# One spreading product per unit instead of two: stacking the high and low parts of the combine weights in a two-layer tower kernel

## What is computed

```python
scores = einsum('btd,de->bte', x, router_w)              # 16 experts
probs = softmax(scores)
routing_weights, routing_idx = top_k(probs, 2)
routing_weights = routing_weights / sum(routing_weights)
combine = einsum('btk,btke->bte', routing_weights, one_hot(routing_idx))   # token x 16, two nonzeros
g = einsum('btd,edf->ebtf', x, gate_w)                   # F = 192 hidden columns an expert
u = einsum('btd,edf->ebtf', x, up_w)
h = silu(g) * u
expert_out = einsum('ebtf,efd->ebtd', h, down_w)
out = einsum('ebtd,bte->btd', expert_out, combine)
```

## Time and profile before

| | |
|---|---|
| median of 3 runs | 296.05 us (294.83 to 296.13) |
| profiled execution | 296.34 us, of which the span is 294.5 us |
| PE busy | 273.1 us, 93% of the span, 1813 matmuls |
| DVE busy | 238.0 us, 81% |
| ACT busy | 147.0 us, 50% |
| POOL busy | 10.0 us, 3% |
| mean granted TensorE clock | 0.984 of full |

### The profile page before, as it was taken

One profiled execution on the slowest core, in us unless ns is written; L12 is line 12 of the kernel. 1 busy time (PEld: TensorE's weight loads), 2 busy tenths in 40 slices (PEclk: granted clock), 3 DMA queues, 4 the chain that ended last, 5 costly groups with the idle time before them and its releaser, 6 DMA issues. The chain is left out here.

```text
span 294.5 us, 4710 instructions
## 1 busy us (share of the span) xinstructions
PE 273.1 (93%) x1813; PEld 237.4 (81%) x1816; DVE 238.0 (81%) x441; ACT 147.0 (50%) x238; POOL 10.0 (3%) x30
## 2 busy tenths in 40 slices
PE   8789399979999999999999999977999999999993
PEld 3445265869999999999999989766899989999862
DVE  1969998897996999899898856799668895878683
ACT  2898750106655664555655433322147773673630
POOL 0200000020000000000000005000000000000000
PEclk9999959999999999999999999999999999999998
DMA  6950499916171755546300085094000000000003
GB/s 234 419 213 19 146 364 434 425 76 212 49 277 26 298 164 189 221 146 240 115 0 3 0 323 249 16 378 178 0 2 0 0 3 0 2 1 2 0 0 71
DMA packets 6567, 40.47 MB, mean 137 GB/s; under 512 B 1169, under 2 KB 1425, under 8 KB 5266
## 3 DMA queue, kind: packets, MB, share of 16 engines
q1 hardware_dynamic: 6546, 40.18, 36.4%
HBM read 39.13 MB, written 0.52 MB: 135 GB/s over the span
## 5 line engine op out<-in xcount | busy, mean ns | idle before, releaser
L876 PE MATMUL bank<-s_xt_hi,s_gu_hi 128*128 128x256 f32 x120 | 34.0, 283 | 0.0
L877 PE MATMUL bank<-s_xt_lo,s_gu_hi 128*128 128x256 f32 x120 | 33.9, 283 | 0.0
L878 PE MATMUL bank<-s_xt_hi,s_gu_lo 128*128 128x256 f32 x120 | 33.9, 282 | 0.0
L994 PE MATMUL bank<-s_xf_hi,s_f_lo 128*128 128x256 f32 x128 | 31.1, 281 | 0.0
L994 PE MATMUL bank<-s_xf_hi,s_f_hi 128*128 128x256 f32 x128 | 31.1, 281 | 0.0
L459 ACT CAST s_xt_hi<-bank 128x512 fp32r<-128x512 f32 x10 | 5.9, 587 | 40.6 <-PE bank L668 34.9
L1515 DVE TENSOR_TENSOR s_f_lo<-s_ffn_raw,s_f_hi 128x1024 fp32r<-128x1024 f32 x16 | 19.6, 1225 | 6.1 <-ACT s_f_hi L592 6.1
L994 PEld LDWEIGHTS bank<-s_xf_hi,s_f_hi 128*128 128x128 f32 x128 | 24.1, 188 | 0.4
L994 PEld LDWEIGHTS bank<-s_xf_hi,s_f_lo 128*128 128x128 f32 x128 | 24.1, 188 | 0.3
L877 PEld LDWEIGHTS bank<-s_xt_lo,s_gu_hi 128*128 128x128 f32 x120 | 23.0, 191 | 0.2
L876 PEld LDWEIGHTS bank<-s_xt_hi,s_gu_hi 128*128 128x128 f32 x120 | 23.0, 191 | 0.3
(11 more groups left out here) (253 smaller groups left out, 713.1 us busy)
## 6 DMA issues: line engine op xcount, KB each, us to landing
s_moe_raw<-moe_gu SPq DMA_DIRECT2D x16, 768.0 KB, 5.9
s_ffn_raw<-ffn_w SPq DMA_DIRECT2D x4, 2048.0 KB, 9.8
s_moe_raw<-moe_dn SPq DMA_DIRECT2D x8, 768.0 KB, 4.4
s_big_raw<-att_w SPq DMA_DIRECT2D x4, 1024.0 KB, 8.7
s_big_raw<-down_w SPq DMA_DIRECT2D x1, 4096.0 KB, 25.2
s_l_raw<-l_w SPq DMA_DIRECT2D x1, 2560.0 KB, 15.2
out<-s_h SPq DMA_DIRECT2D x4, 128.0 KB, 2.3
s_tok_w<-tok_w SPq DMA_DIRECT2D x1, 256.0 KB, 2.7
```

What stands on the lines that cost most here:

```text
L876: pe.matmul(dst, w_hi, xt_hi[:, k, :], start=(k == 0), stop=False)
L877: pe.matmul(dst, w_hi, xt_lo[:, k, :], start=False, stop=False)
L878: last = pe.matmul(dst, w_lo, xt_hi[:, k, :], start=False, stop=(k == KC - 1))
L994: pe.matmul(tb(j, n)[:, 0:TOK], M[w][j][:, k, n * P:(n + 1) * P], M["xf_hi"][:, k, :], start=(w == "w_hi" and k == 0), stop=False)
```

## The change

The high and the low part of the combine matrix are put into different rows of one tile `ct`: high in rows 0 to 15, low in rows 32 to 47 (`CT_LOW = 32`). For this the last routing operation writes the combine matrix three times beside each other (`top3`, 48 columns a tile), so that the transpose delivers it in rows 0 to 15, 16 to 31 and 32 to 47. ACT rounds all 48 rows, DVE replaces rows 32 to 47 by the rest. `ident_r` gets a second one in each column, 32 rows lower, and `sel` is copied from it. Rows 16 to 31 meet only zeros. One matmul then sums high and low part.

```diff
+        CT_LOW = 32
...
-                B["top"] = sb("top", [P, 8, TILES, E], F32, s2)
+                B["top"] = sb("top", [P, 7, TILES, E], F32, s2)
+                B["top3"] = sb("top3", [P, TILES, CT_LOW + E], F32, s2)
...
-                B["ct_hi"] = sb("ct_hi", [P, TOK], F32R, s2)
-                B["ct_lo"] = sb("ct_lo", [P, TOK], F32R, s2)
+                B["ct"] = sb("ct", [P, TOK], F32R, s2)
...
-            pool.tensor_copy(ident_r[:], ident[:, 0:E]).then_inc(con_ready, 1)
+            pool.tensor_tensor(ident_r[:], ident[:, 0:E], ident[:, CT_LOW:CT_LOW + E], ALU.add).then_inc(con_ready, 1)
...
-            pool.memset(B["ct_hi"][:].bitcast(F32), 0.0).then_inc(ct_clear, 1)
-            pool.memset(B["ct_lo"][:].bitcast(F32), 0.0).then_inc(ct_clear, 1)
+            pool.memset(B["ct"][:].bitcast(F32), 0.0).then_inc(ct_clear, 1)
...
-            act.copy(B["sel"][:], ident[:, 0:E].unsqueeze(2).to_broadcast([P, E, P // 2])).then_inc(sel_ready, 1)
+            act.wait_ge(con_ready, 3)
+            act.copy(B["sel"][:], ident_r[:].bitcast(F32).unsqueeze(2).to_broadcast([P, E, P // 2])).then_inc(sel_ready, 1)
...
-            act.wait_ge(ct_clear, 2)
-            act.copy(B["ct_hi"][0:E, :], bank[0][0:E, 0:TOK]).then_inc(cth_ready, 1)
+            act.wait_ge(ct_clear, 1)
+            act.copy(B["ct"][0:CT_LOW + E, :], bank[0][0:CT_LOW + E, 0:TOK]).then_inc(cth_ready, 1)
...
-                pe.matmul(cb_of(n), pick, B["ct_hi"][:], start=True, stop=False)
-                pe.matmul(cb_of(n), pick, B["ct_lo"][:], start=False, stop=True).then_inc(cb_done, 1)
+                pe.matmul(cb_of(n), pick, B["ct"][:], start=True, stop=True).then_inc(cb_done, 1)
...
-                last = pe.transpose(bank[0][0:E, t * P:(t + 1) * P], B["top"][:, 7, t, :], ident)
+                last = pe.transpose(bank[0][0:CT_LOW + E, t * P:(t + 1) * P], B["top3"][:, t, :], ident)
...
-            dve.tensor_tensor(top[:, 7], top[:, 6], over_e(tops[:, 5, :]), ALU.mult).then_inc(comb_ready, 1)
+            by3 = B["top3"][:].rearrange("p t (r e) -> p t r e", r=3)
+            dve.tensor_tensor(by3, top[:, 6].unsqueeze(2).to_broadcast([P, TILES, 3, E]),
+                              tops[:, 5, :].unsqueeze(2).unsqueeze(3).to_broadcast([P, TILES, 3, E]), ALU.mult
+                              ).then_inc(comb_ready, 1)
...
-            dve.tensor_tensor(B["ct_lo"][0:E, :], bank[0][0:E, 0:TOK], B["ct_hi"][0:E, :].bitcast(F32), ALU.subtract
-                              ).then_inc(ct_ready, 1)
+            low = B["ct"][CT_LOW:CT_LOW + E, :]
+            dve.tensor_tensor(low, bank[0][CT_LOW:CT_LOW + E, 0:TOK], low.bitcast(F32), ALU.subtract).then_inc(ct_ready, 1)
```

## The result

The changed kernel took 292.21 us in the median of 6 runs (291.74 to 293.83). The kernel before, on the same chip, took 295.52 us (6 runs, 294.65 to 296.83). The ratio is 0.9885, 95% interval 0.986 to 0.9911; the medians lie 3.31 us apart, about 1.1%. The forecast was 293.3 us with a range of 292.3 to 295.1, so the time fell 0.09 us under the range. (One run of the kernel before, at 536.58 us, is left out as disturbed.)

The account below looks back on a forecast made before the run. TensorE's stream of matmuls was taken to pace the expert stage; 24 x 0.1175 = 2.82 us less 0.03 for transposes gave 2.79, taking the median from 296.05 to 293.26, forecast 293.3 us, range 292.3 to 295.1.

Parts of the forecast that it names:

- TensorE bounds the stage: Expert stage, 66 to 176 us: paced by TensorE's matmul stream, busy 109.92 of 110 us; DVE waits for it.
- The price of a matmul: Each of 24 removed spreading products is worth one start-to-start distance, 0.1175 us; sum 2.82, ends 2.79 and 2.88 us.
- Does it arrive: Inputs that TensorE waits for in the expert stage come early enough, so all 24 terms arrive; chance 0.79.
- The room at `dn(1)`: Between DVE's low part ending at 93.87 us and TensorE's block start at 94.61: shrinks from 0.74 to 0.50 us, holds.
- The busiest pair: From 93.9 to 107.7 us, DVE busy 13.66 of 13.8: pair shortens to 13.45, DVE falls 0.2 us back, then regains it.
- a little under 5 us: DVE's waits for the last spreading product of a unit, 5.1 us in nine places before, would remain nearly as long.
- What was added: 48-column transposes +0.03 us; DVE's 96-column routing operation, ACT's 48-row rounding and GpSimd's sum of two slices cost 0.
- Does it last to the end: Behind `dn(7)`, from 176.48 us: the gain lasts, losing about 0.05 us at worst to the feed-forward weight's load.
- The clock did not fall behind the stage: Rival: TensorE's clock falls after the expert stage, giving 295.7 to 299 us; chance 0.05.
- DVE did not hold TensorE up: Rival: DVE takes over the pace, giving 294.3 or 296.0 us; partly given back (DVE or half price) 0.10, nothing left 0.06.
- the median that the forecast starts from: Kernel before: median 296.05 us, 0.29 under the profiled execution; a few runs' median may differ by some tenths.
- the size of the 24 terms: One removed spreading product in each of 24 units of the expert stage, 0.1175 us each, 2.82 us in all.

Follow-up runs that it names:

- the added DVE operation: A maximum over 128x1024 (1.21 us) added on DVE in each of five pairs: stage 106.64 us in the changed kernel, 109.38 in the kernel before.
- the last batch: Changed kernel 292.75 us mean, with product twice 295.84; kernel before with one product 292.80, rebuilt a third time 296.06.
- the filler kernels: 34 filler matmuls in TensorE's pause from 33 to 37.5 us: kernel before 295.72 us (ratio 0.9999), changed kernel 292.13 us.

## Why the prediction was right in its mechanism and wrong in its number

**TensorE bounds the stage: right.** All TensorE gaps and distances are as before, no new wait stands on it, and the length follows the count of products in all profiles: 106.44 to 106.48 us in six profiles with one product a unit, 109.38 to 109.43 us in seven with two (one of them with the added DVE operation).

**The price of a matmul: 2.82 us forecast, 2.94 measured.** I had divided the combines' own row of eight, 0.1175 us each. The units around them run at 0.120: from one unit to the next without a down block the step fell from 3.11 to 2.98 us, 0.13 for one matmul, while the four at the head of the stage brought the forecast 0.47 together. Over all 24 it is 0.1225 us each. The sum was outside my ends of 2.79 to 2.88 by 0.06.

**Does it arrive: right.** The room at `dn(1)` was to shrink from 0.74 to 0.50 us. In the changed kernel DVE's low part ends at 90.34 + 1.76 = 92.10 us and the block starts at 92.60, the counterpart of the earlier trace rows:

```profile
90.34 1.76 DVE L1326 TENSOR_TENSOR s_dn_lo<-s_moe_raw,s_dn_hi 128x1536 fp32r<-128x1536 f32 x1 [0.95 <-ACT s_dn_hi L513]
...
92.60 0.39 PE L675 MATMUL bank<-s_dn_hi,s_ht_hi 128*128 128x512 f32 x1
```

The busiest pair now takes 13.4 us with DVE busy for 13.26, the next 12.9 with 12.14 (counterpart of the earlier trace rows):

```profile
92.10:105.50 13.40, 13.40 (x98) 12.67 (x97) 13.26 (x25) 8.19 (x16) 0.00 (x0) 1.00 0.66 235
105.50:118.40 12.90, 12.90 (x94) 12.17 (x93) 12.14 (x21) 7.62 (x14) 0.00 (x0) 1.00 0.53 184
```

Wrong was the forecast of DVE's waits, "a little under 5 us": they fell to 2.4. DVE's busy time in the stage stayed at 95.4 us (95.5 before) while the stage became 2.94 us shorter, so DVE's idle time had to shrink by as much, and 2.7 us of it came out of these waits.

**What was added: right or a little dear.** The two 48-column transposes cost nothing that the rows can show, from the start of the last product ahead of them to that of the first behind it is 0.26 us before and 0.25 after. DVE's routing operation has 96 columns and takes longer by 0.07 us, which the wait for ACT behind it took up. GpSimd's sum takes 0.22 us instead of 0.20, not 0.68. ACT's rounding of 48 rows takes 0.37 us instead of 0.36, and DVE's low part of the combine matrix ends at 78.0 us, 1.05 us ahead of the first combine. Here are GpSimd's sum and DVE's operation in the changed kernel, in order of time:

```profile
11.58 0.22 POOL L409 TENSOR_TENSOR s_ident_r<-s_con 128x16 fp32r<-128x16 f32 x1
```

```profile
72.24 0.26 DVE L1372 TENSOR_TENSOR s_top<-s_top,s_tops 128x96 f32<-128x96 f32 x1
```

**Does it last to the end: right.** 118.04 and 118.06 us from the end of the stage to the end of the span, and within 0.05 us of that in all kernels of the study. The clock did not fall behind the stage. DVE did not hold TensorE up with 23 further matmuls gone, and did with 92. The filler behind the stage starts at 172.35 us and not at the forecast 173.7 because unit 0 already starts 1.19 us sooner.

**The steps that failed: the median that the forecast starts from with its "some tenths", and the size of the 24 terms.** I wrote that "a median of a few runs can differ by some tenths from the profiled one" and set the low end 1 us under the forecast. The three runs of before had already spread over 1.3 us, and the whole study shows 294.44 to 298.74 us for kernels with two products. Of this scatter the profiles show where it lies: unit 0 starts between 65.66 and 67.28 us, and everything behind it has one length for a given kernel, within 0.1 us. The median of before that I started from, 296.05, lay 1.6 us above the fastest run of its kind; the median of the changed kernel only 0.75 us above its own. The forecast carried the 296.05 over as it stood. The 1.05 us between 293.26 and the measured 292.21 come apart like this: 0.53 is the starting point, since the kernel before had 295.52 in the six runs of the comparison and not 296.05; 0.15 is the sum (2.94 instead of 2.79: 0.12 for the price of a matmul, 0.03 for transposes that cost nothing); the other 0.37, the 3.31 between the medians less the stage's 2.94, no profile places. The miss of 0.09 us under the low end is smaller than each of them: with 2.94 in the sum and the same margin the low end would have been about 292.15, and the time would have lain inside.

**What stays open.** Why the runs with one product sit nearer to their floor. Over the whole study the excess over the stage is 0.1 to 0.7 us by the interval of 3.1 to 3.6. Within the last batch it can't be told from nothing. What the change adds doesn't make it: with and without the additions the means differ by 0.05 us (one product) and 0.2 us (two), which is inside their scatter. No profile shows a part of it behind unit 0. Most of it goes with the mean granted clock, which is on record for nearly every run. Without the filler kernels, and without the first six runs of before, whose clocks aren't recorded:

| mean granted clock | one product: runs, mean us | two products: runs, mean us | apart |
|---|---|---|---|
| 0.992 to 0.994 | 14, 292.27 | 27, 294.97 | 2.70 |
| 0.987 to 0.988 | 10, 292.51 | 41, 295.79 | 3.28 |
| 0.981 to 0.984 | 5, 293.61 | 42, 296.62 | 3.01 |

Among runs of like clock the distance is 3.0 us (rows weighted by their runs, 95% interval by resampling 2.8 to 3.2), near the stage's 2.94, where the plain means of the same runs lie 3.3 apart. The runs with one product had the lowest clock in 5 of 29, those with two in 42 of 110. So the excess goes with executions whose clock was low for longer. This is read from recorded runs and not from an experiment that set the clock, and whether the different shares are chance or hang on the kernel isn't shown.

## What to carry to other kernels

Where an engine is busy without a pause and the others wait for it, a removed instruction is worth one start-to-start distance, taken as the mean over the whole loop around it, and the room of the next engine should be read at each wait before adding up the terms. Two cheap halves of a product whose contraction dimension is mostly empty fit into one by stacking them in its rows. A range around such a sum has to contain the scatter of the parts that the change never touches: compare where the profiled execution and the fastest run stand, and cut two traces at fixed marks before crediting their difference to the change.

## What the runs showed of the hardware

Behind one and the same pause of TensorE the granted clock stood at 1.2 GHz for 6.8 us in two executions, until 42.8 us in one and until 40.5 in the other, and only the first had a wait of DVE of 0.9 us. Four of sixteen profiles had a further low stretch between 13.5 and 18.5 us. Sorted by these places, unit 0 starts at 65.66 to 66.14 us or at 66.64 to 67.28 us, in kernels that do the same work up to there but for filler and two short GpSimd operations. Keeping the clock up in the one pause with filler did not make the medians faster (ratio 0.9999). A weight load of 48 columns in place of 16 was free between full ones: 0.25 against 0.26 us across two of them.
